# A pair's gathers in two bursts of eight, and window loads behind each burst, in the first edge stage of a four-layer graph network

## The reference

```python
h = maximum(layernorm(x), 0)
Wh = h @ W + b
row, col = edge_index                 # src, dst
sc = softplus(deg_coeff[0] * deg_v + deg_coeff[1])
Wr, Wc = Wh[row], Wh[col]
sim = sum(Wr * Wc) / max(|Wr| * |Wc|, EPS)
base = adj_v * sc * (row != col)
prop_pos = segment_sum(base * relu(sim) * Wc, row)
prop_neg = segment_sum(-base * relu(-sim) * Wc, row)
x = x + scale * (coeff[0] * prop_pos + coeff[1] * prop_neg + coeff[2] * Wh)
```

## Time and profile before

| | us |
|---|---|
| median of 3 timed runs | 5184.12 |
| lowest and highest | 5181.92, 5193.49 |
| the profiled execution, its span | 6621.9 |
| the first edge stage in it (48 to 2084) | 2036 |

### The profile page before, as it was taken

One profiled execution on the slowest core, in us unless ns is written; L12 is line 12 of the kernel. 1 busy time (PEld: TensorE's weight loads), 2 busy tenths in 40 slices (PEclk: granted clock), 3 DMA queues, 4 the chain that ended last, 5 costly groups with the idle time before them and its releaser, 6 DMA issues. The chain is left out here.

```text
span 6621.9 us, 101200 instructions
## 1 busy us (share of the span) xinstructions
PE 4686.8 (71%) x28712; PEld 3011.7 (45%) x28712; DVE 4162.0 (63%) x7696; ACT 1910.3 (29%) x6351; POOL 3158.1 (48%) x2950
## 2 busy tenths in 40 slices
PE   4777777777777666666566666664777777739999
PEld 2333333333334333333445444453444444418998
DVE  4445445444446666666566666664676766688998
ACT  2333333333333000000233333331000000016775
POOL 5333333433332655555344544442566666615554
PEclk6878788887878888888587888776998888969998
DMA  3222222222221111111111111111343334411111
GB/s 98 54 52 52 51 54 55 54 53 52 53 51 32 40 42 36 42 39 34 26 39 41 40 38 41 40 38 35 107 110 107 111 108 119 112 52 49 49 49 36
DMA packets 493009, 379.51 MB, mean 57 GB/s; under 512 B 345991, under 2 KB 379152, under 8 KB 492888
## 3 DMA queue, kind: packets, MB, share of 16 engines
q1 hardware_dynamic: 395352, 288.65, 15.4%
q0 software_dynamic: 90560, 83.37, 7.0%
q10 hardware_dynamic: 6976, 6.23, 0.3%
HBM read 341.76 MB, written 36.12 MB: 57 GB/s over the span
## 5 line engine op out<-in xcount | busy, mean ns | idle before, releaser
L1066 POOL DMA_INDIRECT edge_src_rows<-table_wh,edge_gather_idx x806 | 784.6, 973 | 1213.6 <-DVE edge_small L1185 928.0
L1095 PE MATMUL edge_sums_ps<-edge_onehot_src,edge_halves 128*128 128x512 bf16 x4840 | 1045.0, 360 | 298.3 <-issue 289.3
L933 POOL DMA_INDIRECT edge3a_src_rows<-table_h,edge3a_gather_idx x808 | 762.6, 944 | 558.0 <-issue 313.4
L2096 PE MATMUL edge3a_z_ps<-Wz,edge3a_both_ends_t 128*128 128x396 f32 x1616 | 698.2, 582 | 357.2 <-DVE edge3a_terms L2189 318.0
L1171 DVE TENSOR_SCALAR edge_onehot_src<-layer_node_row,edge_src_col,edge_magnitude 128x1568 bf16<-128x1568 f16 x605 | 412.5, 683 | 845.8 <-remote 583.4
L933 POOL DMA_INDIRECT table_cat<-table_hn,table_gather_idx x592 | 598.1, 1010 | 636.1 <-PE edge_cat_t_ps L1776 344.4
L1457 POOL DMA_INDIRECT edge_src_rows<-table_h,edge_gather_idx x608 | 607.6, 999 | 532.9 <-issue 182.1
L1095 PEld LDWEIGHTS edge_sums_ps<-edge_onehot_src,edge_halves 128*128 128x128 f16 x4840 | 427.6, 104 | 864.3 <-issue 525.0
L2189 DVE SCALAR_TENSOR_TENSOR edge3a_terms<-edge3a_z_ps,att_z 128x792 f32<-128x792 f32 x404 | 385.6, 977 | 401.4 <-DMA edge_edge_attr<-in_ea 219.0
L2096 PEld LDWEIGHTS edge3a_z_ps<-Wz,edge3a_both_ends_t 128*128 128x128 f32 x1616 | 334.0, 217 | 660.5 <-DVE edge3a_terms L2189 364.6
L2508 PE MATMUL edge3b_sums_ps<-edge3b_onehot,edge3b_weighted 128*128 128x128 f32 x4848 | 572.3, 278 | 6.4 <-DVE layers_accT L2546 4.6
(11 more groups left out here) (366 smaller groups left out, 8334.3 us busy)
## 6 DMA issues: line engine op xcount, KB each, us to landing
edge_dst_row<-in_dst_row SPq DMA_DIRECT2D x102, 512.0 KB
edge3a_dst_row<-in_dst_row SPq DMA_DIRECT2D x102, 512.0 KB
edge_window<-table_wh SPq DMA_DIRECT2D x816, 32.5 KB
edge3a_window<-table_h SPq DMA_DIRECT2D x816, 32.0 KB
edge_edge_attr<-in_ea SPq DMA_DIRECT2D x101, 256.0 KB
kept_rows<-edge3a_src_rows SPq DMA_DIRECT2D x101, 256.0 KB
edge3b_src_rows<-kept_rows SPq DMA_DIRECT2D x101, 256.0 KB
edge_edge_attr<-in_ea SPq DMA_DIRECT2D x101, 128.0 KB
```

Of the source, the lines that this page charges most:

```text
L933: nc.gpsimd.indirect_dma_start(self.slot(b, j), None, self.table[:, :], bass.IndirectOffsetOnAxis(ap=self.idx[b][:, j:j + 1], axis=0)).the ...
L1066: nc.gpsimd.indirect_dma_start(g[q][:, j, :], None, k.t_wh[:, :], bass.IndirectOffsetOnAxis(ap=idx[q][:, j:j + 1], axis=0)).then_inc(gathe ...
L1095: mm = pe.matmul(acc[:, i, 0:w], halves[q][:, j, a, :, :].rearrange("p h d -> p (h d)"), hot[:, o:o + w], start=first and a == 0, stop=False)
L2096: mm = pe.matmul(zp[q % 2][:, i, 0:H * ZH], hcT[h][:, j * P:(j + 1) * P], k.Wz[:, :], start=True, stop=True)
```

## The change

It does three things. The 16 gathers of a pair become two bursts of eight, each with its own semaphore for each buffer (`gathered[q][h]`). Ahead of its first burst POOL waits until PE has used the first tile of pair t-3, and ahead of the second until it has used six of DVE's tiles of that pair, the last of which is tile 6. And SP waits, ahead of each eight window loads, until that half's gathers have landed. The source numbers are loaded one pair earlier in SP's order, ahead of the loads of the pair before. DVE waits for both halves where it waited for one semaphore. No compute instruction is added or removed, and the numbers of DMAs stay the same.

```diff
--- before.py
+++ after.py
@@ -180,6 +180,11 @@
 def tiles_of(t):
 
     return min(2 * B, -(-E // P) - t * 2 * B) if isinstance(t, int) else 2 * B
+
+
+def half_of(t, h):
+
+    return max(0, min(B, tiles_of(t) - h * B))
 
 
 def more(t, ahead):
@@ -1013,7 +1018,7 @@
         wc_ps = c.ps("dst_rows_ps", [P, 512])
         acc = c.ps("sums_ps", [P, 4, 512])
         idx_loaded = [c.sem(f"idx_loaded{q}") for q in (0, 1)]
-        gathered = [c.sem(f"gathered{q}") for q in (0, 1)]
+        gathered = [[c.sem(f"gathered{q}_half{h}") for h in (0, 1)] for q in (0, 1)]
         rows_loaded = [c.sem(f"rows_loaded{h}") for h in (0, 1)]
         win_loaded = [c.sem(f"window_loaded{q}") for q in (0, 1)]
         (oht_ready, wc_ready, wc_read, hi_ready, lo_ready, hot_v, hot_a, used_v, used_a, away_done,
@@ -1040,15 +1045,23 @@
         with nc.Block() as block:
             @block.sync
             def _(sp):
+                def numbers(t, q, m):
+                    for h in (0, 1):
+                        wait_past(sp, gathered[q][h], 16 * B * m)
+                    sp.dma_start(idx[q][:, :], k.src_t[:, bass.ds(t * PB, PB)]).then_inc(idx_loaded[q], 16)
+
+                numbers(0, 0, 0)
+
                 def body(t, q, m):
-                    wait_past(sp, gathered[q], 16 * PB * m)
-                    sp.dma_start(idx[q][:, :], k.src_t[:, bass.ds(t * PB, PB)]).then_inc(idx_loaded[q], 16)
+                    if more(t, 1):
+                        numbers(t + 1, 1 - q, m + q)
                     for h in (0, 1):
                         wait_past(sp, oht_ready, 2 * t + h - 1)
                         sp.dma_start(drow[h][:, :], k.dst_row[bass.ds(2 * t + h, 1), :].to_broadcast([P, ROWS])
                                      ).then_inc(rows_loaded[h], 16)
                     wait_past(sp, wc_ready, 3 * t - 3)
                     for h in (0, 1):
+                        sp.wait_ge(gathered[q][h], 16 * (B * m + half_of(t, h)))
                         for j, base in enumerate(window_starts(nc, k, SP, t, h)):
                             sp.dma_start(win[q][:, h * B + j, :], k.t_wh[bass.ds(base, P), :]
                                          ).then_inc(win_loaded[q], 16)
@@ -1063,9 +1076,12 @@
 
                     pool.sem_inc(gate, 1)
                     for j in range(tiles_of(t)):
+                        if j % B == 0:
+                            wait_past(pool, used_v, NV * (t - 3) + 5 * j // B + 1)
+                            pool.sem_inc(gate, 1)
                         nc.gpsimd.indirect_dma_start(
                             g[q][:, j, :], None, k.t_wh[:, :],
-                            bass.IndirectOffsetOnAxis(ap=idx[q][:, j:j + 1], axis=0)).then_inc(gathered[q], 16)
+                            bass.IndirectOffsetOnAxis(ap=idx[q][:, j:j + 1], axis=0)).then_inc(gathered[q][j // B], 16)
                 by_parity(pool, body)
 
             @block.tensor
@@ -1172,7 +1188,8 @@
                                       mag[q][:, j:j + 1], ALU.is_equal, ALU.mult).then_inc(hot_v, 1)
 
                 def products(t, q, m):
-                    dve.wait_ge(gathered[q], 16 * (PB * m + tiles_of(t)))
+                    for h in (0, 1):
+                        dve.wait_ge(gathered[q][h], 16 * (B * m + half_of(t, h)))
                     dve.wait_ge(wc_read, 3 * t + 3)
                     dve.tensor_tensor(prod, g[q][:, :, 0:D], wcs[q][:, :, 0:D],
                                       ALU.mult).then_inc(prod_done, 1)
```

## The result

| | us |
|---|---|
| after: median of 4 runs, lowest to highest | 5582.95, 5580.86 to 5588.16 |
| before, on the same chip | 5185.1, 5181.92 to 5193.49 |
| after / before | 1.0769, 95% interval 1.0756 to 1.0782 |

The account below looks back on a forecast made before the run. PE was taken to bound the first edge stage at 25.3 us a pair; a 28.1 us chain adds 132 us and the start 33, so 165 on 5184 gives 5349 us, range 5050 to 5450.

Parts of the forecast that it names:

- the chain: First edge stage, PE through POOL and SP back to PE: 28.1 us a turn against 25.3, 132 us over 47 pairs.
- PE to the end of tile 6: 9.4 us: Chain term: PE from a pair's expansion start to the end of tile 6, with durations from a fast stretch.
- rival 3: Chain longer, by windows slowed by the next first burst or PE slower after pauses: 5457 us and more, chance 0.05.
- first to the eighth gather: 8.7 us: Chain term: POOL issuing a burst of eight, seven spacings of 1.25 us.
- I take 1.25, the only spacing seen: Gather spacing on POOL taken as 1.25 us, over the bound of 0.94.
- the loads' 9.0 for 9.2: Chain terms from eighth gather to PE: 2.5 us to a consumer, then 6.7 us for SP's windows until PE.
- The start: Stage start: pair 2's windows, now behind 48 gathers, ready at 118.4 instead of 85.7, 33 us more.
- Before, undisturbed: 85.7: Time in us at which the old kernel's PE, without the loss, would reach pair 2's expansion.
- the loss of 13.6 us: First edge stage: PE's loss per profiled pair (38.9 against 25.3 us), taken as likeliest absent from timed runs.
- Rival 1: Share r of PE's profiled loss is real when timed: 571 r - 165 us won, 2 us a pair remaining; chance 0.32.
- POOL's waits lie in gaps of an engine that needs 20 of 25 us: POOL's extra increments and waits were counted as costing nothing.
- its 5235: Bound in us with gathers at 0.94 us: chain 25.9, pairs costing 28, start about 23.

Follow-up runs that it names:

- windows_free: Changed kernel without SP's wait for landed gathers ahead of the window loads, both bursts and gates kept, short kind: 5202.38 us, 1.0023 of before.
- warm_2: Changed kernel plus 20 throwaway matmuls of constants ahead of PE's first expansion of each pair, short kind: 5452.0 us, 1.0514 of before.
- after_3: The changed kernel, unchanged, on a chip of the long kind: 6327.89 us against 6605.86 for before, 0.9578.
- after_low_2: Changed kernel whose second burst also waits until DVE's `low` is done, long kind: 6369.54 us, 0.964 of before.
- windows_free_2: Changed kernel without SP's wait for landed gathers, run again on another chip of the short kind: 5202.23 us, 1.0033 of before.
- numbers_only: Changed kernel without SP's wait for gathers and POOL's waits on PE's progress, short kind: 5205.63 us, 1.0033 of before.
- gate_tile4: Changed kernel with the second burst released after four of DVE's tiles (tile 4) instead of six, short kind: 5483.06 us, 1.0566 of before.
- gathers_free: Changed kernel without POOL's waits on PE's progress ahead of the bursts, SP's wait kept, short kind: 5281.57 us, 1.0186 of before.
- after_2: The changed kernel, unchanged, on another chip of the short kind: 5587.14 us against 5184.7 for before, 1.0774.
- windows_free_3: Changed kernel without SP's wait for landed gathers, on a chip of the long kind: 6088.12 us, 0.9221 of before.

## Why the prediction was wrong

- **The direction and the chain were right.** The forecast was a chain over PE, POOL, SP and back, and one wait removed (windows_free) brings a pair from 33.1 back to 25.2 us. What failed is the size of the turn: 28.1 us predicted, 33.1 measured. The wait sits where the prediction put it, at PE's expansion, once a pair.
- **The term "PE to the end of tile 6: 9.4 us" was mis-sized.** It is 12.6. I took the durations from a fast stretch, and dismissed the slower PE in rival 3 because "2.8 us is a short one". But the other term below makes the pause longer, and at 4.8 us PE comes back at clock 0.54. Pauses of 3.66 and 3.43 us brought it to 0.50, one of 0.99 did not; what a pause of 2.8 does was not measured. warm_2 measures this term: 2.9 us a pair (33.1 to 30.2), 135 us in all.
- **The term "first to the eighth gather: 8.7 us" was mis-sized.** It is 11.0. "I take 1.25, the only spacing seen" was the failure: the earlier trace rows shows a burst of 16 of the long kind, in which DVE hardly works (1.58 us of 13.8 in the earlier trace rows), so no gather met DVE's long operations. In the same place after_3, on the long kind too, has 11.0 again: what matters is where the burst lies. On its own the term adds 2.3 us a pair, 108 us; after_low_2 ties 1.4 of them to `low`. With POOL's 1.0 for 0.8 and the loads' 9.0 for 9.2, a turn is 33.5 in the timeline for 28.1.
- **The start was mis-sized the other way: 33 us predicted, 16 measured** against a kernel without SP's wait. In after the first sums begin at 109.0 and pair 2's expansion at 126.4, where 118.4 was predicted. But "Before, undisturbed: 85.7" was too early: in windows_free_2 the first sums begin at 94.5 and pair 2's expansion at 110.5, since PE then waits for one-hot matrices and for windows too, and in numbers_only, without either of the change's waits, that expansion begins at 110.8. Before itself has no trace on the short kind. The first row is after's, the second that of windows_free_2:

```profile
126.39 2.82 PE L1096 MATMUL edge_dst_rows_ps<-edge_window,edge_onehot_t 128*128 128x65 f32 x12 [12.69 <-DMA edge_window<-table_wh]
```

```profile
110.45 2.82 PE L1095 MATMUL edge_dst_rows_ps<-edge_window,edge_onehot_t 128*128 128x65 f32 x12 [3.38 <-DMA edge_window<-table_wh]
```

- **Sum.** In products, after's last one is 389 us later than that of windows_free_2 (1727.0 and 1338.0), about what 47 pairs at 7.9 us and the 16 of the start give (387); the spans differ by 381.5. With the 17 us of numbers_only this is the 398. Predicted were 132 and 33.
- **The step that the loss of 13.6 us is "not in a timed run" was right for the timed chip and wrong in its cause.** I gave it to the profiler. Before takes 6610 us timed as well as profiled on the long kind. Rows of one kind had been set beside times of the other. The consequence for the 5184 us was the same, by luck of which chip served the timed runs: on the long kind the sign turns (0.9578).
- **Rival 1's price** of 2 us a pair for what is left of the slow stretches was too high (none is left). Its formula at r = 1 gives 406 us won, with 278 measured. With none of the 2 us left (94 us more) and a chain 5.0 us a pair longer (235 us less) it comes to 265.
- **"POOL's waits lie in gaps of an engine that needs 20 of 25 us"** was wrong: in windows_free_2 and numbers_only it has no gap over 0.3 us. It did no harm to the sum, but gate_tile4 missed by it, and probably gathers_free.
- **A slip in the bounds.** With gathers of 0.94 us the prediction's terms give a turn of 26.0 us, not 25.9; that moves its 5235 by 5 us and decides nothing.

The Trainium skill, "DMA: Bandwidth & Descriptors", section "Rules for kernel authors" (issue early, wait late), agrees with the runs: taking out SP's early wait alone wins 385 us on the short kind (after_2 and windows_free_2) and 240 on the long kind (after_3 and windows_free_3).

Open are the 17 us of numbers_only, what makes a chip one of the long kind, whether it stays so, and why the second, third and fourth big stages are longer on it too (819, 1053 and 1033 us against the earlier trace rows); I tried nothing on them.

## What to carry to other kernels

Before reading a loss out of a trace, ask whether the trace and the times belong together: a trace much longer than the timed runs is a warning, and a run of the old kernel with both on one chip tells it. When a change closes a loop through several engines, take each term as it will be inside that loop: PE behind a pause, gathers beside DVE's long operations. And put the wait on a gather at its consumer, not ahead of loads that don't need it.

## What the runs showed of the hardware

- Two kinds of chip: the same kernel takes 5185 to 5188 us on some and 6606 to 6612 on others, each chip having been measured in one set. On the latter, once eight gathers of a burst of 16 are issued, PE does 13 matmuls in 13.8 us; a burst of eight with a gap doesn't bring that on in the first stage.
- An indirect gather takes POOL 0.94 us alone, 3.15 when it begins during a 128x2048 f32 operation of DVE (`weighted`), 2.7 during one that writes f16 (`low`), and 1.4 to 1.75 when it begins 0.3 to 0.6 us into the 128x1024 `spread`; one that began together with `spread` took 0.95. Sixteen gathers with these fill 25.2 us.
- After 4.8 us of idling PE ran 7.4 us at a granted clock of 0.54, and after 3.66 and 3.43 us it was at 0.50; 20 throwaway matmuls in the pause kept it at 1.00, and so did a pause of only 0.99 us.
